# Four cross-attention layers with feed-forward blocks: norm statistics taken behind the additions to x, rounding passes moved into layer 1, projections at other steps

## The reference

```python
def norm(x): return (x - mean(x)) / sqrt(var(x) + 1e-5)
x = x + L0_attention(norm(x), ctx)   # one head of 256, own norms with gain and bias, biases
x = x + L0_ffn(norm(x))              # router over 8, experts 0 and 1 only, silu
x = x + L1_attention(norm(x), ctx)   # 8 heads of 128; every token sees all 3000 keys of the context
x = x + L1_ffn(norm(x))              # gate, up, down with weights rounded to -1, 0, 1
x = x + L2_attention(norm(x), ctx)   # 16 heads of 64; 112 tokens see the 375 keys of their batch
x = x + L2_ffn(norm(x))              # top 2 of 8 experts, each two matrices without a nonlinearity between
x = x + L3_attention(norm(x), ctx)   # as layer 2
x = x + L3_ffn(norm(x))              # top 2 of 8 experts and a shared one, silu

def weight_quant(w):                 # in L1_ffn, for each of three matrices
    scale = 1.0 / clip(mean(abs(w)), 1e-5)
    return clip(round(w * scale), -1, 1) / scale
```

## Time and profile before

| | us |
|---|---|
| median of three runs | 1853.04 |
| lowest and highest | 1852.96, 1857.46 |
| the profiled execution's own time | 1855.11 |
| its span | 1853.3 |

### The profile page before, as it was taken

One profiled execution on the slowest core, in us unless ns is written; L12 is line 12 of the kernel. 1 busy time (PEld: TensorE's weight loads), 2 busy tenths in 40 slices (PEclk: granted clock), 3 DMA queues, 4 the chain that ended last, 5 costly groups with the idle time before them and its releaser, 6 DMA issues. The chain is left out here.

```text
span 1853.3 us, 30977 instructions
## 1 busy us (share of the span) xinstructions
PE 1736.2 (94%) x11311; PEld 1531.8 (83%) x11311; DVE 1392.1 (75%) x3082; ACT 1037.3 (56%) x2275; POOL 638.1 (34%) x906
## 2 busy tenths in 40 slices
PE   7878999999999999999888899999969999999699
PEld 6657899998989999989866788888857888888598
DVE  6467787777878687878677677767878788888775
ACT  4355555655655655555555555656641667776542
POOL 0613030110303030302100455555661467666542
PEclk9988999999999999999989999999989999999899
DMA  5110000000000000000020121110000000000021
GB/s 175 44 42 27 1 4 9 1 12 1 13 1 13 1 12 1 16 1 1 1 91 32 62 74 55 61 56 26 10 1 18 9 16 19 15 10 4 24 58 43
DMA packets 17751, 49.04 MB, mean 26 GB/s; under 512 B 2617, under 2 KB 7362, under 8 KB 15938
## 3 DMA queue, kind: packets, MB, share of 16 engines
q1 hardware_dynamic: 16738, 46.25, 7.6%
q10 hardware_dynamic: 864, 0.83, 0.1%
HBM read 46.15 MB, written 0.92 MB: 25 GB/s over the span
## 5 line engine op out<-in xcount | busy, mean ns | idle before, releaser
L1381 ACT ACTIVATE a_pH<-banks 125x512 fp32r<-125x512 f32 (+1 forms) x384 | 203.5, 544 | 268.0 <-PE banks L195 191.4
L1452 DVE TENSOR_TENSOR a_pL<-banks,a_pH 125x512 fp32r<-125x512 f32 (+1 forms) x384 | 235.5, 623 | 116.6 <-ACT a_pH L1381 114.6
L2011 POOL TENSOR_TENSOR a_prob<-a_prob,a_rinv 112x750 f32<-112x750 f32 x128 | 184.0, 1437 | 196.0 <-DVE a_rinv L2334 195.8
L1433 DVE TENSOR_SCALAR_CACHE_REDUCE a_prob<-banks 128x500 f32<-128x500 f32 x336 | 221.8, 677 | 5.0 <-PE banks L195 4.1
L1225 POOL TENSOR_TENSOR a_head_oH<-a_o,ones 128x256 fp32r<-128x256 f32 (+1 forms) x24 | 16.4, 684 | 605.6 <-DVE a_o L1460 605.6
L1271 PE MATMUL banks<-ident,a_prob 128*125 128x128 f32 x1344 | 201.2, 274 | 6.6 <-ACT a_prob L1366 4.4
L1366 ACT ACTIVATE a_prob<-a_prob,a_nmax 128x1000 f32<-128x1000 f32 x168 | 187.9, 1120 | 32.9 <-DVE a_nmax L1436 32.9
L195 PE MATMUL banks<-a_pH,a_head_vH 125*128 125x256 f32 (+1 forms) x576 | 200.1, 347 | 5.2 <-DVE a_pL L1452 4.3
L1271 PEld LDWEIGHTS banks<-ident,a_prob 128*125 128x125 f32 x1344 | 186.4, 188 | 9.8 <-ACT a_prob L1366 4.9
L195 PE MATMUL banks<-a_pH,a_head_vL 125*128 125x256 f32 (+1 forms) x576 | 173.0, 300 | 0.0
L195 PE MATMUL banks<-a_pL,a_head_vH 125*128 125x256 f32 (+1 forms) x576 | 172.5, 299 | 0.0
(11 more groups left out here) (413 smaller groups left out, 4869.4 us busy)
## 6 DMA issues: line engine op xcount, KB each, us to landing
a_w_out<-in_f_out SPq DMA_DIRECT2D x6, 1024.0 KB, 4.8
a_w_in<-in_f_in SPq DMA_DIRECT2D x12, 512.0 KB, 4.7
f_raw<-in_f_w SPq DMA_DIRECT2D x9, 513.0 KB, 3.6
pair_raw<-in_a_qk SPq DMA_DIRECT2D x16, 256.0 KB, 2.7
pair_raw<-in_a_w SPq DMA_DIRECT2D x8, 384.0 KB, 3.2
a_v<-in_ctx_rows SPq DMA_DIRECT2D x4, 576.0 KB, 7.5
a_kT<-in_f_w SPq DMA_DIRECT2D x2, 1024.0 KB, 5.9
pair_raw<-in_a_wv SPq DMA_DIRECT2D x8, 256.0 KB, 3.2
```

Of the source, the lines that this page charges most:

```text
L1381: act.activation(pH[:, c % RING, 0:wide], TB[c % 4][0:KB, 0:wide], ACT.Copy).then_inc(t_high, 1)
L1433: dve.tensor_scalar(prob[:, at, c * CHUNK:(c + 1) * CHUNK], SB[c % 3][:, 0:CHUNK], SCALE, None, ALU.mult, ALU.max, accum_out=chunk_max[:, ...
L1452: dve.tensor_tensor(pL[:, c % RING, 0:wide], TB[c % 4][0:KB, 0:wide], pH[:, c % RING, 0:wide].bitcast(F32), ALU.subtract).then_inc(t_done, 1)
L2011: pool.tensor_tensor(both, both, rinv[:, n % RING, :].unsqueeze(2).to_broadcast([SEQ, 2, KEYS]), ALU.mult).then_inc(p_normed, 1)
```

## The change

1. The buffers of the norm are shared by all stages. Each stage takes `bn_stats` and `bn_aggr` of each tile behind the addition that finishes the tile, and the next stage starts with the variance. The Sqrt table is loaded at the end of a stage; ScalarE does the root ahead of its copies.
2. In layer 0's attention, the scores of batches 0 and 1 come ahead of the last value unit, the addition of the output bias to x is split over steps 1 and 2, and the output tiles 0 to 4 go into steps 3 to 7. Scaling and rounding of the feed-forward weights are taken out of it. Only the sums of absolute values and the mean stay.
3. Scaling and rounding go into layer 1's attention as 12 pieces of 512 columns, two for each of heads 0 to 5: SyncE loads them, VectorE scales and rounds them between the chunks of the head's third group, and ScalarE writes them between its value units.
4. In layers 2 and 3 the tables read otherwise, and in layer 2 the expert products are spread over two pairs.

```diff
+def next_norm_stats(dve, s, q, i, added, value):
+    dve.wait_ge(added, value)
+    dve.bn_stats(s.ln.stats[:, i, :], s.x[:, i, :]).then_inc(q.stats, 1)
+def next_norm_aggr(dve, s, q, i):
+    dve.wait_ge(q.stats, i + 1)
+    dve.bn_aggr(s.ln.mean_var[:, i, :], s.ln.stats[:, i, :]).then_inc(q.aggr, 1)
 def layer_norm_vector(dve, b, q, src, dst):
-    layer_norm_roots(dve, b, q, src)
+    layer_norm_roots(dve, b, q)
     layer_norm_apply(dve, b, q, src, dst)
...
@@ layer0_attention @@
+    SCORES_AT = KTILES // 2 - 1
+    BIAS_AT = {1: range(0, 4), 2: range(4, TILES)}
+            def add_tile(i):
+                dve.wait_ge(y_filled, i + 1)
+                dve.tensor_tensor(s.x[:, i, :], s.x[:, i, :], YB[i][:, 0:D], ALU.add).then_inc(y_added, 1)
+                if i >= 1:
+                    next_norm_stats(dve, s, qn, i - 1, y_added, i)
+                if i >= 2:
+                    next_norm_aggr(dve, s, qn, i - 2)
...
-            act.wait_ge(cut_done, 3 * PIECES)
-            for m in range(3):
-                act.wait_ge(quant_clipped, m + 1)
-                act.activation(s.w_quant[:, m, :], quant_raw[m], ACT.Copy, bias=-MAGIC).then_inc(quant_done, 1)
+            act.wait_ge(abs_total, 1)
+            act.activation(s.w_mean[:], B[4][:, 0:3], ACT.Copy, scale=1.0 / (P * QUANT)).then_inc(mean_ready, 1)
+            load_table(act, s, ACT.Sqrt, n=2)
...
+                if b >= 3:
+                    output_tile(b - 3)
             mix(BATCH - 1)
...
@@ layer1_attention @@
+    QUANT_SCALE_AT, QUANT_ROUND_AT = (1, 3), (5, 7)
+    QUANT_OUT_AT = (1, 2)
+            def quant_out(h, n):
+                piece = QUANT_RING * h + n
+                act.wait_ge(quant_rounded, piece + 1)
+                act.activation(s.quant_pieces[:, piece, :], s.quant_raw[:, n, :], ACT.Copy, bias=-MAGIC).then_inc(q.quant_done, 1)
+def quant_loads(sp, s, q, dram_f1, h):
+    need(sp, q.quant_done, QUANT_RING * h)
+    for n in range(QUANT_RING):
+        m, part = divmod(QUANT_RING * h + n, 2048 // QUANT_PIECE)
+        sp.dma_start(s.quant_raw[:, n, :], dram_f1[:, m, part * QUANT_PIECE:(part + 1) * QUANT_PIECE]).then_inc(q.quant_loaded[n], 16)
...
-            add_outputs(dve, s, q, TB, base(HEADS), rinv)
+            add_last_outputs(dve, s, q, qn, TB, base(HEADS), rinv)
...
@@ layers 2 and 3, attention @@
-    KEYS_AT = (2, 4, 5, 6, 7, 9)
-    QUERIES_AT = (3, 8)
-    OUT_AT = (4, 6, 8, 9)
-    EXPERTS_AT = {1: (0, 0), 3: (0, 1), 5: (1, 0), 7: (1, 1)} if experts else {}
-    VALUES_AT = (1, 2, 3, 3, 4, 5, 5, 6, 6, 7, 8, 8) if experts else (2, 3, 3, 5, 5, 7, 7, 10, 11, 11, 13, 13)
+    KEYS_AT = (2, 4, 5, 6, 8, 9)
+    QUERIES_AT = (3, 7)
+    OUT_AT = [(6, 8, 9, 10)] * (HEADS - 1) + [(4, 6, 8, 9)]
+    EXPERTS_AT = {3: (0, 0), 7: (0, 1), 11: (1, 0), 15: (1, 1)} if experts else {}
+    VALUES_AT = (1, 2, 4, 4, 5, 6, 8, 9, 10, 12, 13, 14) if experts else (2, 3, 4, 5, 7, 8, 9, 10, 11, 12, 13, 14)
...
+            for t in range(4):
+                next_norm_stats(dve, s, qn, t, done, number["o", HEADS - 1, t // 2] + 1)
+            for t in range(4):
+                next_norm_aggr(dve, s, qn, t)
             for g in range(2, GROUPS):
                 outs(HEADS - 1, g)
+                for t in range(part_tiles(g).start, part_tiles(g).stop):
+                    next_norm_stats(dve, s, qn, t, done, number["o", HEADS - 1, g] + 1)
+            for t in range(4, TILES):
+                next_norm_aggr(dve, s, qn, t)
...
@@ layer 2, feed-forward @@
-        ROOTS_AT = 3
+        ROOTS_AT = 0
```

248 lines of the change are left out of this document (165 added, 83 removed).

## The result

Six runs of each kernel on one chip gave a median of 1844.44 us for the changed kernel (1842.47 to 1846.56) and 1855.22 for the one before (1852.96 to 1857.46): a ratio of 0.9943, 95% interval 0.9930 to 0.9956. It is faster, by 10.8 us, where 17 were forecast, and 1.4 us above the range. The profiled execution took 1845.55 with a span of 1843.8, against 1853.3 before: -9.5. The difference is best read stage by stage. A stage's length is the distance between the first instruction of any engine behind one barrier and the first behind the next. "Clock loss" is the span times (1 - the granted clock over it). It counts all time at the lower clock level, also where nothing waited for TensorE.

A forecast was written before the change was run, and what follows sets the result against it. TensorE, busy 94% of the span, was taken as the bound, with gains at its waits and stage ends and starts; terms summed to -17.1 from 1855.11, giving 1838.0, less 2.07 for the median: 1836.0 us, range 1829.5 to 1843.

The forecast's parts named there:

- Layer 0's attention, -9.6: Layer 0's attention: earlier scores, split bias, tiles inside the loop and a shorter tail save 9.6 us (-7 to -10.5).
- I let the lead grow to 3.4 by step 3: Layer 0's attention loop: first turning 1.6 us sooner, then another 0.6 from each of three steps.
- The table load: Layer 0's attention tail: load counted at 1.28 us; with the skill's extra drain the stage's term would be -8.3.
- Rounding in layer 1, +2.5: Layer 1's attention: ScalarE's copies let 0.4 us a head reach TensorE, VectorE's inserts nothing; +2.5 us (0 to +4).
- Layer 2's attention, -5.5 in all: Layer 2's attention: start 2.4 us back, tables -4.5, tail 1.4 longer.
- gives 2.4 back: Layer 2's start: TensorE's 1.34 us wait for the norm and the chain behind it give 2.4 us.
- I work out 0.5 in layer 3 and 2.2 in layer 2: Attention tables of layers 2 and 3: moving parts from full steps into light ones saves 2.2 and 0.5 us.
- Start of layer 3, -2.0: Start of layer 3's attention: the norm without its statistics gives 2.0 us.
- Its tables, -4.6: Layer 3's attention: seven waits for queries removed at 0.58 us each, 4.1, plus 0.5 from evening out.
- The norms pay in full: Rival on all stage starts: seven savings of 2.96 us with free tails; half the difference allowed, 1826 us; chance 0.1.
- The loops give nothing: Rival on the attention loops: tables give 2 us, layer 0's loop grows to its upper bound; 1845.6 us; chance 0.15.
- Slower: Rival on layer 1: copies hold up the values' chain; decisive from 4.2 us a head, 1863 at 5; chance 0.02.

The follow-up runs named there:

- e5: Changed kernel with layer 0's output tiles all behind the attention loop again, split bias and early scores kept; that stage took 102.37 us, 3.55 less.
- e6: Changed kernel with ScalarE's two copies of rounded weights per head moved from value units 1 and 2 to 10 and 11; layer 1's attention 0.8 us shorter.
- e4: Changed kernel with the end of layer 1's attention and start of its feed-forward as before; attention -2.2 us, feed-forward -0.7.
- e3: Changed kernel plus six products nobody reads in the idle tail of layer 1's feed-forward; layer 2's attention 3.8 us shorter.
- e7: Changed kernel plus products nobody reads at the end of every stage but the last; span 5.9 us shorter.
- e1: Changed kernel with layer 2's first expert product back at step 1 instead of 3; layer 2's attention 2.8 us shorter.
- e8: Changed kernel with all statistics back at the stages' starts, tables kept; span 1839.2 us, ratio 0.9920 to the kernel before.
- e12: Changed kernel unaltered, profiled again; layer 2's feed-forward 51.65 us and layer 3's attention 311.07, against 52.98 and 312.63.
- e2: Changed kernel with all tables of layers 2 and 3 as before; layer 3's attention 317.5 us, layer 2's 356.6; ratio 0.9981 to the kernel before.
- e9: Changed kernel with statistics behind additions only ahead of the feed-forwards of layers 2 and 3; span 1840.2 us.
- e13: Changed kernel with statistics and tables both as before, leaving layer 0's attention and layer 1's rounding changed; twelve runs between 1848.1 and 1858.8 us.
- e11: Edits of e1, e3, e5, e6 and e9 joined, plus products nobody reads in four more places; median 1832.19 us, ratio 0.9872 to the kernel before.

## Why the prediction was wrong

The direction and many single terms stood; the sum was 7.6 us too favourable. Another 1.0 is that I took 2.07 off for a profiled execution slower than the median; the changed kernel's, 1845.55, is only 1.1 above its own.

- **Layer 0's attention, -9.6, measured -7.1: the step that failed is "I let the lead grow to 3.4 by step 3".** It was 1.25. The first turning came 0.6 earlier and not 1.6, and after the second the lead grew no more, as VectorE's scalings took 0.73 to 1.08 us beside GpSimd's work instead of 0.42; I had not asked what GpSimd does in these steps. From the fourth turning to the last it took 17.18 us instead of 12.65, 1.13 more a step and not 1.0 (1.3 in the last two). Of the 2.7 by which the last turning missed its place, 2.15 are the lead. The last turning is at 95.33, later than the 94 that I named as the sign of error. My lower bound, -7, was what came, though not by its cause (a step that grows by 1.7; that sum, four times 0.7, is 2.8 and not 2.6). e5 shows that the tiles in the loop are the dear part.
- **The table load** took 1.28 (103.25), and the next activation starts at 104.55, 0.02 behind its end. ScalarE: Activation LUTs in the Trainium skill, What ACT_TABLE_LOAD costs, states a drain of about 1.38 us besides; this trace shows none. The measured -7.1 is no evidence for it: it comes from the loop.
- **Start of layer 0's feed-forward, 0:** right (5.87 against 5.95, no idle time at the turning). **Its tail, +1.8:** +1.4.
- **Layer 1's start, -1.4:** -1.8 (first scores 10.09 behind the start, 11.90 before). **Rounding in layer 1, +2.5:** about +2, by another split: 0.17 in each of six heads (I had 0.4), which the copies cause (e6), and 1.0 in the first head, from the two small operations on the scale, which I had put at nothing. The last head took 0.9 more, for which the sum had no term. **Layer 1's tail, +2.8:** +3.3, of which the statistics are 2.0 (e4) and the rest clock. **Slower first keys, +0.7:** +0.3.
- **Layer 2's attention, -5.5 in all, measured -1.0: two steps failed.** That the start "gives 2.4 back": 0.5. I had counted a wait that ends as time gained, and not asked what TensorE does just before: it comes out of an idle tail that has grown (2.15 us ahead of the first product, 1.46 before), and its first 30 products run at a granted clock of 0.50 and take 6.14 us; with products in that tail the start gives 1.8 (e3) or 1.5 (e7). "I work out 0.5 in layer 3 and 2.2 in layer 2, where the expert products are moved as well": the product moved from step 1 to 3 was the cover of a wait for `a_o_parts`; e1 gives back 2.8. The clock's fall in the first head goes with that product and not with the start: it never came with the product at step 1, and it came in e7 and e8, whose starts ran at 1.00. (In the timeline the last head's last scores come 2.4 sooner behind the start than before, 336.78 against 339.16: start 0.5, body 1.9, and the tail takes 1.4 of it.)
- **Start of layer 2's feed-forward, -2.5:** -2.7. The root ahead of the copies bounds it, as said. **Tails of 1.4 in layers 2 and 3:** 1.4 each, and 1.0 in the feed-forward.
- **Start of layer 3, -2.0:** -0.8, where the turning again follows the products without idle time. It is layer 2's failure once more: in e12, the same kernel with the clock at 1.00 at this start, it gives 2.4. **Its tables, -4.6:** -4.7, shown apart by e2 (4.9). The size came out by some luck: the 0.58 a wait was taken from two steps that are not alike (the second makes half of the queries and no keys), the waits for queries fell by 2.8 in all where 4.1 was forecast, and where the other 2 come from wasn't traced. And "if only half the waits vanish" the terms give -5.9, not -5. **Its feed-forward, -3.1:** -2.4.
- **The rivals.** *The norms pay in full* is out: with the old tables they were worth 3.3 us, and with the new ones nothing. *The loops give nothing* came close in number (1845.6 against 1844.4), and its half on layer 0, the loop at its upper bound, came true; the half on the tables is out, as they gave 4.9 in layer 3 and 2.1 in layer 2 and not 2 in all. *Slower*: layer 1's copies cost 0.17 a head, not 4.2.

What stays open: what makes the clock fall in one execution and not in another of the same code (e8 and e9, e12, e13's spread; e13's twelve runs on one chip lie 10.7 us apart, so the chip can't be all of it), why e3 and e9 keep it in layer 2's first head, and what the moved statistics are worth by themselves. That the two small operations cause the wait in layer 1's first head is read from the timeline, and no run takes them away.

## What to carry to other kernels

When work goes from a stage's start into the tail of the one before, TensorE is idle for longer at the seam (here 3.73, 2.15 and 2.87 us ahead of three stages, 1.67, 1.46 and 1.92 before), so price the first products behind the seam at the lower clock (6.14 us where they take 3.62 at the full one, in layer 2) before a removed wait is booked as gain. An instruction that is moved "to a lighter step" may be the cover of a wait in the step that it leaves: look in the trace at what ends directly behind it. A one-line operation that moves along with a big one needs a place of its own: two operations on three columns cost 1.0 where they landed. And where stages of identical code differ by 1 to 3 us, run the unchanged kernel once more and read single stages before giving a small difference a cause.

## What the runs showed of the hardware

- Six products of 500 columns whose results nobody reads, 1.59 us in a tail where TensorE had nothing to do, kept the clock at 1.00 instead of 0.50 at the next start, and brought the turning 2.5 us and the second scores 1.3 us nearer (e3; 1.0 in e7). The stage got 3.8 shorter in e3, but only 1.0 in e7, where the clock fell again 29 us on. Filled in the tails of four stages they are part of the fastest kernel (e11). Filling all took 21 us off the clock loss and 5.9 off the span (e7), so most of the loss that went did not lie on the path.
- The same VectorE operation, 375 columns, took 0.57 to 1.12 us where a GpSimd operation under way had 0.35 us or more to run when it began, and ended 0.21 or 0.22 behind that operation each time (eight cases in two kernels); with GpSimd idle it took 0.41 or 0.42.
- Two profiled executions of one kernel differed by 1.33 and 1.56 us in two neighbouring stages, by where the clock's low stretches fell; the values recur as pairs in other kernels.
- A table load on ScalarE took 1.28 us, and the next activation began 0.02 behind its end (103.25, 104.55).
